# Attention rows of maxima sent per pair of heads, maxima of the first sixteen heads placed later

## The chip, the cores and the metric

The kernel runs on one core of a Trainium2 chip. The metric is the time of one execution on the device in microseconds (us); lower is better. Before the change three runs took 604.35, 604.46 and 606.38 us, so the median is 604.46 us.

## The reference

The input x has shape (4, 512, 128): 4 batches of 512 tokens of width 128. What is computed:

```
x  = x + attention(layernorm(x))         # its own two layer norms inside
x  = x + moe(layernorm(x))               # 8 experts, the best 2 of each token

attention(x):                            # 16 heads of 64, one shared key/value head
    xn = ln1(x);  q = xn @ Wq;  k, v = split(xn @ Wkv)
    sim  = q k^T * 64**-0.5              # per batch and head: 512 x 512
    attn = softmax(sim)                  # minus the row's maximum, exp, over the sum
    return ln2((attn v) @ Wo)
```

Only the attention's start is touched by the change: the row maxima of `sim` and how they reach the score matmul.

## The kernel before

All work of the attention is one list of steps, written by `attention_schedule`. Each step has a place (a slot number, then an order inside the slot), the list is sorted by it, and every engine walks the same list and issues only what is its own. So the list fixes the order of work inside each engine, and semaphores fix it between engines. The list counts 64 heads (4 batches of 16), 32 pairs of heads, and four tiles of 128 tokens to a head, so 256 slots. Slot n holds `EXP` n.

The steps around the change:

- `Q` p: TensorE makes the queries of pair p in one PSUM bank `q_ps` with three matmuls (high and low parts of a float32 split, L1205 to L1207). Batch steps `XT`, `K` and `V` use the same bank, and each of them waits until the one before has been read (`bank_read`).
- `QHI` p: ScalarE copies the rounded (high) part into `q_hl`, one instruction to each of the two heads (L1177). `QLO` p: VectorE writes the remainder (low part) into the other half of `q_hl`, two instructions (L1100). GpSimd copies the high parts once more, into `q_hm` (L1021).
- `MAX` k: TensorE multiplies one tile of 128 queries with all keys into one of two banks of `max_ps` (L1270) and VectorE takes the negated maximum over each row, a column of `less_max` (L1115). The matmul of `MAX` k waits until `MAX` k-2 has been reduced. There are four to a head; the first of a head waits for the head's `QLO`.
- `SHIFT` n: VectorE transposes a group's columns of `less_max` with four 32x32 transposes into `mrow` (L1126), and the DMA queue of SyncE writes them as row 64 of `q_hm` (L957), one DMA to a pair of heads. Behind each of the first nine `SHIFT` the same queue issues up to four large writes that blank `sorted_rows` in HBM (L963), which the experts' part needs later.
- `EXP` k: TensorE makes a 128x512 tile of scores with two matmuls, L1290 (from `q_hl`) and L1292 (from `q_hm`, which adds the row of maxima), and ScalarE takes the exponential (L1195). The first `EXP` of a group of heads waits for that group's row DMAs. The matmuls of `EXP` k wait until exponential k-2 is done (two banks of `s_ps`).
- `PV`: matmuls of `prob` with `v` (L1306, four records to a step). `V`, `VC`: values of a batch, made by TensorE and copied by ScalarE.
- `keep_busy`: matmuls on zeros into an unused bank (L1220) that feed nothing; one stands in front of each of `MAX` 2 to 11, five before `MAX` 0 and three before the first `V`.

`shifts` groups the heads: two groups of two heads, then groups of four. `less_max` has two buffers of 32 columns. In slot order the list of before around the start reads:

```
... Q0 QHI0 QLO0 MAX0-4 Q1 MAX5 QHI1 MAX6 MAX7 QLO1 SHIFT0 MAX8-11 Q2 QHI2 QLO2
EXP0 MAX12,13 EXP1 MAX14,15 EXP2 MAX16,17 SHIFT1 EXP3 MAX18,19 Q3 EXP4 MAX20,21 QHI3 QLO3
EXP5 MAX22,23 V VC EXP6 MAX24,25 PV EXP7 MAX26,27 Q4 EXP8 MAX28,29 PV QHI4 QLO4
EXP9 MAX30,31 PV EXP10 MAX32 EXP11 MAX33 PV SHIFT2 EXP12 ...
```

Of the kernel before, what the change touches and what calls it, by code (L numbers as in the profile page):

```python
# [5 lines left out]
F32 = mybir.dt.float32  # L6
# [6 lines left out]
P = 128  # L13
# [3 lines left out]
UH = 8  # L17
UP = UH // 2
JT = 4
# [8 lines left out]
def attention_schedule(units):  # L28

    slots, lead = UH * JT, MAX_LEAD
    placed = []

    def place(slot, order, kind, u, a):
        placed.append((slot, order, (kind, u, a)))

    for n, kind in enumerate(IN_STEPS):

        place(FIRST_V_AT if kind in ("V", "VC") else -1000 + n, 4, kind, 0, 0)
        for b in range(1, units // 2):

            place(2 * slots * (b - 1) + IN_AT[n] + (LATER if b == 1 else 0), 4, kind, b, 0)
    for b in range(units // 2 - 1):
        at, lag = (AFTER_AT, 2) if b < units // 2 - 2 else (LATE_AFTER_AT, 0.25)
        for n, kind in enumerate(AFTER_STEPS):
            place(2 * slots * (b + 1) + at[n], 4, kind, b, 0)  # L60
        for n in range(TOP_K * JT if b < units // 2 - 2 else EARLY_SENDS):
            place(2 * slots * (b + 1) + at[AFTER_STEPS.index("PLACE")] + lag * n, 4.5, "SEND", b, n)
    for pair in range(units * UP):
        u, p = divmod(pair, UP)

        at = (-30, -11, *FIRST_Q_AT)[pair] if pair < 4 else 8 * pair - 19 - lead
        place(at, 3, "Q", u, p)
        place(at + 1, 3, "QHI", u, p)

        place(-8 if pair == 1 else at + 1, 4, "QLO", u, p)  # L70
        for jt in range(JT):
            place(8 * pair + PV_AT[jt], 2, "PV", u, p * JT + jt)
        place(8 * pair + PV_AT[-1] + 1, 1, "RAW", u, p)
    for n in range(units * slots):
        u, a = divmod(n, slots)
        place(n, 0, "EXP", u, a)
        place(n - 15 if n < 12 else (n - 12) // 2 if n < 32 else n - 16 - lead, 1, "MAX", u, a)
    for n, (head, _) in enumerate(shifts(units)):
        place(FIRST_SHIFT_AT[n] if n < 2 else JT * head - lead + 1, 3, "SHIFT", n, 0)
    for u in range(units):  # L80
        after = slots * (u + 1)
        if u < units - 1:
            place(after + SUM_AT[0], 5, "SUM", u, 0)
            place(after + SUM_AT[1], 5, "SUM", u, 1)
            for n, kind in enumerate(RECIP_STEPS):
                place(after + RECIP_AT[n], 5, kind, u, 0)
            for c in range(UP):
                place(after + NORM_AT[c], 5, "NORM", u, c)
                place(after + NORM_AT[c] + OUT_LAG, 5, "OUT", u, c)
        else:  # L90

            for c, at in enumerate(LAST_SUM_AT):
                place(after + at, 6, "SUM", u, c)
            for n, (kind, a) in enumerate(LAST_STEPS):
                place(after + LAST_SUM_AT[1] + 1, 9 + n, kind, u, a)
    return [step for _, _, step in sorted(placed, key=lambda entry: entry[:2])]
# [27 lines left out]
LAST_STEPS = (("SUMS", 0), ("SPREAD", 0), ("RECIP", 0), ("GATHER", 0), ("NORM", 0), ("NORM", 1), ("OUT", 0),  # L124
              ("NORM", 2), ("OUT", 1), ("NORM", 3), ("OUT", 2), ("OUT", 3))

FIRST_Q_AT = (-3, 3)

FIRST_SHIFT_AT = (-7.5, 2)

FIRST_V_AT = 5

LATER = 8

VECTOR_HEADS = (7,)

# [5 lines left out]

def shifts(units):

    return [(0, 2), (2, 2)] + [(head, 4) for head in range(4, units * UH, 4)]


EXPERTS = 8  # L150
# [28 lines left out]
def bass_preln_mqa_moe_kernel(nc, x, ln1_g, ln1_b, wq, wkv, wo, ln2_g, ln2_b, gate_wT, gate_upT, downT,  # L179
# [32 lines left out]
    with ExitStack() as whole:  # L212
# [659 lines left out]
        with ExitStack() as att:  # L872
# [15 lines left out]
            wkl = sb(att, "wkl", [P, P], F32R)  # L888
            wvh = sb(att, "wvh", [P, DH], F32R)
            wvl = sb(att, "wvl", [P, DH], F32R)  # L890
            less_max = sb(att, "less_max", [P, 2, 32], F32R)
            mrow = sb(att, "mrow", [32, 2, P], F32R)
            prob = sb(att, "prob", [P, 4, JT, S])
            fold = sb(att, "fold", [P, 2, S])
# [28 lines left out]
            @block.sync  # L923
            def _(sp):
                sp.dma_start(x1[:, 0:TPB, :], x_t[0]).then_inc(x1_in[0], 16)
                for dst, src in ((ident[:, :], eye), (gcol[:, :], ln1_g.rearrange("(p o) -> p o", o=1)),
                                 (bcol[:, :], ln1_b.rearrange("(p o) -> p o", o=1)),
                                 (sumsel[:, :, :], sum_rows)):
                    sp.dma_start(dst, src).then_inc(consts_in, 16)
                sp.dma_start(wk_raw[:, 0:DH], wkv[:, 0:DH]).then_inc(wkv_in, 16)  # L930
                sp.dma_start(wk_raw[:, DH:P], wkv[:, 0:DH]).then_inc(wkv_in, 16)
                sp.dma_start(wv_raw, wkv[:, DH:2 * DH]).then_inc(wkv_in, 16)
                sp.dma_start(wq_raw, wq).then_inc(wq_in, 16)
                sp.dma_start(wof[:, :, :], wo.rearrange("(c p) n -> p c n", p=P)).then_inc(wo_in, 16)
                for half in range(2):
                    for part in range(2):
                        row = part * LOW_ROW + half * UH // 2
                        sp.dma_start(hs_raw[row:row + UH // 2, :, :],
                                     head_rows[half + 2 * part:P:32, :, :]).then_inc(hs_in, 16)
                for b in range(1, NB):  # L940
                    sp.dma_start(x1[:, b * TPB:(b + 1) * TPB, :], x_t[b]).then_inc(x1_in[b], 16)
                for dst, src in ((g2[:, :], ln2_g.partition_broadcast(P)), (b2[:, :], ln2_b.partition_broadcast(P)),
                                 (gw[:, :], gate_wT), (tri[:, :, :], lower)):
                    sp.dma_start(dst, src).then_inc(consts2_in, 16)
                for kind, u, a in steps:
                    tail_sync(sp, kind, u)
                    if kind == "SHIFT":
                        head, heads = shift_heads[u]

                        sp.wait_ge(mrow_ready, u + 1)  # L950
                        if head >= Q_SLOTS:

                            sp.wait_ge(score_mm, (head + heads - Q_SLOTS) * JT)
                        for h in range(0, heads, 2):
                            slot = (head + h) % Q_SLOTS
                            first = (head % 4 + h) * JT
                            sp.dma_start(q_hm[DH:DH + 1, slot:slot + 2, :].bitcast(F32),  # L957
                                         mrow[first:first + 2 * JT, u % 2, :].bitcast(F32)).then_inc(mrow_in[u % 2], 16)

                        if u == 0:  # L960
                            sp.wait_ge(blank_set, 1)
                        for n in range(4 * u, min(4 * u + 4, FILLS)):
                            sp.dma_start(sorted_rows[n * S:(n + 1) * S, :].rearrange("(p r) c -> p r c", r=TPB),  # L963
                                         blank[:, :, :]).then_inc(rows_filled, 16)
                    if kind == "V" and u == NB - 1:
                        sp.wait_ge(rows_filled, 16 * FILLS)
                        for e in range(E):
                            load_gate_up(sp, e)
                sp.wait_ge(tiles_ready, 1)
                sp.wait_ge(rows_sent, 16 * TOP_K * TPB * (LB - 1))  # L970
                for k in range(EARLY_ROWS):
                    load_rows(sp, k, xs_early[:, k, :])
# [88 lines left out]
            def _(dve):  # L1061
                nc.vector.memset(kly[DH:DH + 1, :, :].bitcast(F32), 1.0).then_inc(ones_set, 1)
                link(dve, nc.vector.memset(less_max[:, :, :].bitcast(F32), 0.0))
                for kind, u, a in steps:
# [38 lines left out]
                    if kind == "MAX":  # L1103
                        k = u * UH * JT + a
                        head, it = divmod(k, JT)
                        group, i = divmod(head, 4)
                        dve.wait_ge(max_mm, k + 1)
                        col = i * JT + it
                        if i == 0 and it == 0 and group >= 2:

                            dve.wait_ge(mrow_ready, group)
                        if head == 2 and it == 0:

                            dve.wait_ge(mrow_ready, 1)
                        nc.vector.tensor_reduce(less_max[:, group % 2, col:col + 1], max_ps[:, k % 2, :], AX_X,  # L1115
                                                ALU.max, negate=True).then_inc(max_done, 1)
                    if kind == "SHIFT":
                        head, heads = shift_heads[u]
                        group = head // 4
                        dve.wait_ge(max_done, (head + heads) * JT)  # L1120
                        if u >= 2:

# [1 line left out]
                        for n in range(P // 32):  # L1124
                            part = slice(32 * n, 32 * n + 32)
                            last = nc.vector.transpose(mrow[:, u % 2, part].bitcast(F32),  # L1126
                                                       less_max[part, group % 2, :].bitcast(F32))
                        last.then_inc(mrow_ready, 1)
                    if kind == "EXP" and a % JT >= 1 and vector_sums(u * UH + a // JT):

# [71 lines left out]
            def _(pe):  # L1202
# [23 lines left out]
                for kind, u, a in steps:  # L1226
# [33 lines left out]
                    if kind == "MAX":  # L1260
                        i, it = divmod(a, JT)
                        k = u * UH * JT + a
                        if it == 0:
                            pe.wait_ge(q_lo, u * UH + i + 1)
                        if 2 <= k < 12:
                            keep_busy(BUSY["rows"])
                        if k >= 2:

# [544 lines left out]
```

## Time and profile before

| | before |
|---|---|
| median of 3 runs | 604.46 us |
| profiled execution, its own time | 608.39 us |
| span of its trace | 606.6 us |
| mean granted TensorE clock | 0.984 of full speed |
| TensorE matmul busy | 571.6 us |
| VectorE busy | 398.2 us |
| ScalarE busy | 296.9 us |
| GpSimd busy | 395.7 us |

The profile's PE is TensorE's matmuls, PEld its weight loads, DVE is VectorE, ACT ScalarE, POOL GpSimd, and SPq the DMA queue of SyncE. PE's busy time is an outline of pipelined matmuls, so a busy PE may still lose time between them. PEclk 1.00 is the full clock of 2.4 GHz, 0.50 the half clock of 1.2 GHz.

### The profile page before, as it was taken

What the parts mean: (1) busy time and instruction counts of PE and PEld (TensorE: products, weight loads), DVE (VectorE), ACT (ScalarE), POOL (GpSimd) and SP (SyncE); (2) the same over time, 40 slices, a digit from 0 to 9 for tenths busy, and PEclk for the clock granted to TensorE, in tenths of its full rate; (3) what the DMA queues carried; (4) which work ended last, traced back from release to release, by engine and by line L of the source; (5) the groups of instructions that cost most, each with busy time, mean ns of one, the idle gap of its engine ahead of it and who ended that gap; (6) DMA issues with size and microseconds to landing.
All of it is one profiled execution on the core that took longest, in us unless ns stands there. A gap on an engine that the chain in (4) does not pass through costs nothing. (4 is left out here: it accounts for less than half of the span.)

```text
span 606.6 us, 8802 instructions
## 1 busy us (share of the span) xinstructions
PE 571.6 (94%) x2543; PEld 325.6 (54%) x2543; DVE 398.2 (66%) x873; ACT 296.9 (49%) x559; POOL 395.7 (65%) x329
## 2 busy tenths in 40 slices
PE   8799999999999999998999999899997878999992
PEld 6464455444545454444545445344433567788881
DVE  4878656657756869774676878875584468444453
ACT  3235655445636564553655455355536553444550
POOL 5438776667758866799696579849747934445333
PEclk9889999999999999999999999899999999999997
DMA  5111011010201200071000000000005300231033
GB/s 166 71 72 71 2 71 71 5 72 1 75 1 72 74 2 1 7 243 69 1 5 0 2 7 21 13 2 4 11 0 151 94 23 27 58 81 52 23 126 98
DMA packets 27518, 29.46 MB, mean 49 GB/s; under 512 B 7732, under 2 KB 18742, under 8 KB 27473
## 3 DMA queue, kind: packets, MB, share of 16 engines
q1 hardware_dynamic: 24912, 24.27, 12.6%
q0 software_dynamic: 2272, 4.24, 2.1%
q8 instruction: 23, 0.38, 0.3%
q10 hardware_dynamic: 288, 0.39, 0.2%
q14 instruction: 23, 0.18, 0.1%
HBM read 13.50 MB, written 15.32 MB: 48 GB/s over the span
## 5 line engine op out<-in xcount | busy, mean ns | idle before, releaser
L1195 ACT ACTIVATE prob<-s_ps 128x512 f32<-128x512 f32 x256 | 150.8, 599 | 183.3 <-PE s_ps L1292 180.7
L1115 DVE TENSOR_REDUCE less_max<-max_ps 128x1 fp32r<-128x512 f32 x256 | 174.0, 689 | 82.5 <-PE max_ps L1270 79.7
L1041 POOL TENSOR_TENSOR fold<-prob 128x1024 f32<-128x1024 f32 x63 | 149.9, 2380 | 88.3 <-ACT prob L1195 87.6
L1306 PE MATMUL pv_ps<-prob,v 128*64 128x512 f32 x512 | 138.5, 621 | 0.0
L1290 PE MATMUL s_ps<-q_hl,khh 128*128 128x512 f32 x256 | 117.9, 461 | 0.7 <-ACT prob L1195 0.7
L1270 PE MATMUL max_ps<-khh,q_hl 128*128 128x512 f32 x256 | 103.0, 408 | 5.3 <-DVE less_max L1115 4.7
L1292 PE MATMUL s_ps<-q_hm,kly 65*128 65x512 f32 x256 | 101.8, 398 | 0.0
L1290 PEld LDWEIGHTS s_ps<-q_hl,khh 128*128 128x128 f32 x256 | 48.6, 190 | 86.2 <-ACT prob L1195 67.0
L1047 POOL TENSOR_TENSOR psums<-fold 128x512 f32<-128x512 f32 x63 | 80.9, 1285 | 4.9
L1270 PEld LDWEIGHTS max_ps<-khh,q_hl 128*128 128x128 f32 x256 | 49.1, 192 | 23.4 <-DVE less_max L1115 11.0
L1292 PEld LDWEIGHTS s_ps<-q_hm,kly 65*128 65x128 f32 x256 | 48.8, 191 | 9.2 <-issue 3.4
L1306 PEld LDWEIGHTS pv_ps<-prob,v 128*64 128x64 f32 x512 | 25.6, 135 | 46.2 <-issue 34.5
L497 POOL DMA_INDIRECT sorted_rows<-xr,place_i x32 | 34.7, 1084 | 22.4 <-issue 12.7
L1100 DVE TENSOR_TENSOR q_hl<-q_ps,q_hl 64x512 fp32r<-64x512 f32 x64 | 44.1, 689 | 6.3 <-ACT q_hl L1177 4.9
L1514 DVE TENSOR_TENSOR ha<-up_ps,gl 128x512 f32<-128x512 f32 x39 | 26.9, 690 | 29.4 <-PE up_ps L1651 13.6
L1177 ACT ACTIVATE q_hl<-q_ps 64x512 fp32r<-64x512 f32 x64 | 37.6, 587 | 12.4 <-PE q_ps L1207 11.5
L1475 POOL DMA_INDIRECT parts<-raw,psums x22 | 22.2, 1011 | 29.1 <-DVE raw L1523 23.6
L787 DVE TENSOR_TENSOR ao<-sum_ps,raw 128x512 f32<-128x512 f32 x32 | 22.1, 690 | 27.2 <-PE sum_ps L853 27.1
L1021 POOL TENSOR_SCALAR q_hm<-q_hl 64x1024 fp32r<-64x1024 f32 x32 | 33.4, 1043 | 8.6 <-ACT q_hl L1177 8.6
L1588 ACT ACTIVATE ht<-q_ps 128x512 f32<-128x512 f32 x39 | 23.3, 597 | 27.2 <-PE q_ps L1660 24.5
L863 PE MATMUL y_ps<-ao,wof 128*128 128x512 f32 x64 | 35.9, 646 | 0.0
L1673 PE MATMUL sum_ps<-wd,ht 128*128 x216 | 29.2, 278 | 5.0 <-DVE raw L1523 2.7
(251 smaller groups left out, 769.8 us busy)
## 6 DMA issues: line engine op xcount, KB each, us to landing
sorted_rows<-raw_w SPq DMA_DIRECT2D x36, 260.0 KB, 2.6
raw_w<-in_gate_upT SPq DMA_DIRECT2D x8, 512.0 KB, 9.2
wd<-in_downT SPq DMA_DIRECT2D x8, 256.0 KB
raw_w<-parts SPq DMA_DIRECT2D x7, 256.0 KB, 3.2
psums<-sorted_rows SPq DMA_DIRECT2D x22, 65.0 KB, 1.7
x<-in_x SPq DMA_DIRECT2D x4, 256.0 KB, 4.4
xs_first<-sorted_rows SPq DMA_DIRECT2D x15, 65.0 KB, 1.8
out<-x SPq DMA_DIRECT2D x3, 256.0 KB, 2.3
```

The lines of the kernel that those rows point to most:

```text
L497: nc.gpsimd.indirect_dma_start(out=sorted_rows, out_offset=bass.IndirectOffsetOnAxis(ap=place_i[:, n, t:t + 1], axis=0), in_=xr[:, n, t, : ...
L863: nc.tensor.matmul(y_ps[:, :], wof[:, c, :], ao[:, k % 2, :], start=c == 0, stop=c == PAIRS - 1).then_inc(out_mm, 1)
L1041: nc.gpsimd.tensor_tensor(fold[:, :, :], prob[:, head % 4, 0:2, :], prob[:, head % 4, 2:4, :], ALU.add).then_inc(prob_folded, 1)
L1047: nc.gpsimd.tensor_tensor(psums[:, head % SUM_SLOTS, :], fold[:, 0, :], fold[:, 1, :], ALU.add).then_inc(head_sum, 1)
L1100: nc.vector.tensor_tensor(q_hl[DH:P, h % Q_SLOTS, :], q_ps[DH * hd:DH * hd + DH, :], q_hl[0:DH, h % Q_SLOTS, :].bitcast(F32), ALU.subtract ...
L1115: nc.vector.tensor_reduce(less_max[:, group % 2, col:col + 1], max_ps[:, k % 2, :], AX_X, ALU.max, negate=True).then_inc(max_done, 1)
L1177: nc.scalar.activation(q_hl[0:DH, (2 * k + hd) % Q_SLOTS, :], q_ps[DH * hd:DH * hd + DH, :], ACT.Copy).then_inc(q_hi, 1)
L1195: nc.scalar.activation(prob[:, head % 4, jt, :], s_ps[:, k % 2, :], ACT.Exp, scale=SCALE).then_inc(exp_done, 1)
L1270: nc.tensor.matmul(max_ps[:, k % 2, :], q_hl[:, k // JT % Q_SLOTS, it * P:(it + 1) * P], khh[:, b % 2, :], start=True, stop=True).then_inc ...
L1290: nc.tensor.matmul(s_ps[:, k % 2, :], khh[:, b % 2, keys], q_hl[:, slot, :], start=True, stop=False)
L1292: nc.tensor.matmul(s_ps[:, k % 2, :], kly[0:DH + 1, b % 2, keys], q_hm[0:DH + 1, slot, :], start=False, stop=True).then_inc(score_mm, 1)
L1306: last = nc.tensor.matmul(pv_ps[DH * hd:DH * hd + DH, :], v[:, b % 2, jt, :], prob[:, head % 4, jt, :], start=(jt == 0), stop=(jt == JT - 1))
```

## The change

- The first sixteen heads are shifted in eight groups of two (before: two, two, four, four, four). Later groups still hold four heads. `less_max` gets a third buffer, and each group takes the next one in turn.
- `MAX` 10 to 63 are placed at 0.78 of a slot each from slot 0 on. Before, `MAX` 12 to 31 stood two to a slot and one to a slot followed.
- `SHIFT` 0 now stands ahead of `QLO` 1 (the low parts of the second pair).
- `Q` 2 moves from before `EXP` 0 to behind it, `Q` 3 from slot 3 to 4, and `SHIFT` 1 from slot 2 to 4.5.
- The single `keep_busy` matmuls stand in front of `MAX` 2 to 9 only, two fewer.

```diff
-        place(-8 if pair == 1 else at + 1, 4, "QLO", u, p)
+        place(-7.4 if pair == 1 else at + 1, 4, "QLO", u, p)
...
-        place(n - 15 if n < 12 else (n - 12) // 2 if n < 32 else n - 16 - lead, 1, "MAX", u, a)
+        place(n - 15 if n < 10 else 0.78 * (n - 10) if n < 64 else n - 16 - lead, 1, "MAX", u, a)
...
-FIRST_Q_AT = (-3, 3)
+FIRST_Q_AT = (0, 4)
-FIRST_SHIFT_AT = (-7.5, 2)
+FIRST_SHIFT_AT = (-7.5, 4.5)
...
+MAX_SLOTS = 3
...
-    return [(0, 2), (2, 2)] + [(head, 4) for head in range(4, units * UH, 4)]
+    return [(head, 2) for head in range(0, 16, 2)] + [(head, 4) for head in range(16, units * UH, 4)]
...
-            less_max = sb(att, "less_max", [P, 2, 32], F32R)
+            less_max = sb(att, "less_max", [P, MAX_SLOTS, 32], F32R)
...
-                            first = (head % 4 + h) * JT
+                            first = h * JT
...
-                        group, i = divmod(head, 4)
+                        n = max(n for n, (first, _) in enumerate(shift_heads) if first <= head)
                         dve.wait_ge(max_mm, k + 1)
-                        col = i * JT + it
-                        if i == 0 and it == 0 and group >= 2:
-                            dve.wait_ge(mrow_ready, group)
-                        if head == 2 and it == 0:
-                            dve.wait_ge(mrow_ready, 1)
-                        nc.vector.tensor_reduce(less_max[:, group % 2, col:col + 1], max_ps[:, k % 2, :], AX_X,
+                        col = k - shift_heads[n][0] * JT
+                        if col == 0 and n >= MAX_SLOTS:
+                            dve.wait_ge(mrow_ready, n - MAX_SLOTS + 1)
+                        nc.vector.tensor_reduce(less_max[:, n % MAX_SLOTS, col:col + 1], max_ps[:, k % 2, :], AX_X,
...
-                                                       less_max[part, group % 2, :].bitcast(F32))
+                                                       less_max[part, u % MAX_SLOTS, :].bitcast(F32))
...
-                        if 2 <= k < 12:
+                        if 2 <= k < 10:
                             keep_busy(BUSY["rows"])
```

The list after the change reads:

```
... Q0 QHI0 QLO0 MAX0-4 Q1 MAX5 QHI1 MAX6 MAX7 SHIFT0 QLO1 MAX8,9
EXP0 MAX10 Q2 MAX11 EXP1 QHI2 QLO2 MAX12 EXP2 MAX13 EXP3 MAX14,15 EXP4 Q3 SHIFT1 MAX16
EXP5 QHI3 V VC QLO3 MAX17 EXP6 PV MAX18 EXP7 Q4 MAX19,20 EXP8 PV QHI4 QLO4 MAX21
EXP9 PV MAX22 EXP10 MAX23,24 EXP11 PV SHIFT2 MAX25 EXP12 ... SHIFT3 behind EXP19, SHIFT4
behind EXP27, SHIFT5 behind EXP35, SHIFT6 behind EXP43, SHIFT7 behind EXP51
```

From slot 42 on the two lists hold the same steps at the same places, but for the numbering of the shifts and one more shift of two heads in slot 51.

## Rows read from the trace of the kernel before

**Rows 1.** Busy time of each engine over the span.
```profile
PE 571.6 (94%) x2543; PEld 325.6 (54%) x2543; DVE 398.2 (66%) x873; ACT 296.9 (49%) x559; POOL 395.7 (65%) x329
```

**Rows 2.** By stretches: bounds, length, busy time (instructions) by engine, clock, DMA, GB/s.
```profile
20.00:30.00 10.00, 6.68 (x20) 4.30 (x18) 8.04 (x16) 2.61 (x5) 2.53 (x7) 0.83 0.28 107
30.00:40.00 10.00, 9.03 (x31) 5.88 (x31) 9.04 (x18) 3.51 (x7) 4.73 (x4) 0.83 0.24 91
...
160.00:200.00 40.00, 40.00 (x172) 20.92 (x168) 23.68 (x44) 20.27 (x39) 29.71 (x24) 1.00 0.08 28
```

**Rows 3.** Waits from 45 to 120 us: in total, times, longest.
```profile
PEld max_ps L1270 <- DVE less_max L1115: 0.2, 1, 0.2
```

**Rows 4.** Timeline of PE, 20 to 31 us: start, length, what [idle before].
```profile
20.37 0.49 PE L1270 MATMUL max_ps<-khh,q_hl 128*128 128x512 f32 x1
22.36 0.50 PE L1220 MATMUL y_ps<-q_hm 128*128 128x512 f32 x1 [1.50 <-DVE q_hl L1100]
...
24.75 0.80 PE L1270 MATMUL max_ps<-khh,q_hl 128*128 128x512 f32 x1 [0.96 <-DVE less_max L1115]
...
27.48 0.58 PE L1290 MATMUL s_ps<-q_hl,khh 128*128 128x512 f32 x1
...
28.59 0.39 PE L1290 MATMUL s_ps<-q_hl,khh 128*128 128x512 f32 x1
28.83 0.39 PE L1292 MATMUL s_ps<-q_hm,kly 65*128 65x512 f32 x1
30.53 1.28 PE L1270 MATMUL max_ps<-khh,q_hl 128*128 128x512 f32 x2 [1.32 <-DVE less_max L1115]
```

**Rows 5.** Timeline of DVE, 19 to 33 us.
```profile
19.63 1.97 DVE L1115 TENSOR_REDUCE less_max<-max_ps 128x1 fp32r<-128x512 f32 x3 [0.46 <-PE max_ps L1270]
21.63 1.41 DVE L1100 TENSOR_TENSOR q_hl<-q_ps,q_hl 64x512 fp32r<-64x512 f32 x2
23.07 0.84 DVE L1126 STREAM_TRANSPOSE mrow<-less_max 32x32 f32<-32x32 f32 x4
...
28.35 1.41 DVE L1100 TENSOR_TENSOR q_hl<-q_ps,q_hl 64x512 fp32r<-64x512 f32 x2 [1.21 <-ACT q_hl L1177]
29.79 2.75 DVE L1115 TENSOR_REDUCE less_max<-max_ps 128x1 fp32r<-128x512 f32 x4
```

**Rows 6.** Timeline of ACT, 27 to 31 us.
```profile
27.72 1.22 ACT L1177 ACTIVATE q_hl<-q_ps 64x512 fp32r<-64x512 f32 x2 [7.34 <-PE q_ps L1207]
28.96 1.08 ACT L1195 ACTIVATE prob<-s_ps 128x512 f32<-128x512 f32 x2
```

**Rows 7.** Row DMAs: issues on SPq, and the one score matmul released by them.
```profile
23.93 0.78 SPq L957 DMA_DIRECT2D q_hm<-mrow  x1
...
260.43 1.38 SPq L957 DMA_DIRECT2D q_hm<-mrow  x2
...
264.19 0.19 PEld L1290 LDWEIGHTS s_ps<-q_hl,khh 128*128 128x128 f32 x1 [0.19 <-DMA q_hm<-mrow]
```

**Rows 8.** Stretches of 1 us, the clock's column third from the end.
```profile
24.00:25.00 1.00, 0.25 (x1) 0.25 (x2) 0.99 (x2) 0.00 (x0) 0.00 (x0) 0.73 0.00 0
...
27.00:28.00 1.00, 1.00 (x4) 0.77 (x3) 0.13 (x1) 0.28 (x1) 0.00 (x0) 0.57 0.99 383
...
31.00:32.00 1.00, 0.91 (x3) 0.72 (x3) 0.92 (x3) 0.00 (x0) 0.00 (x0) 0.64 0.00 0
...
34.00:35.00 1.00, 1.00 (x4) 0.65 (x4) 0.96 (x5) 0.59 (x1) 0.00 (x0) 0.65 0.03 8
```

**Rows 9.** Timeline of PE, 39 to 40 us, the first V.
```profile
39.27 0.30 PE L1205 MATMUL q_ps<-wvh,xh 128*128 128x64 f32 x1 [0.24 <-DVE q_hl L1100]
```

**Rows 10.** Timeline of PE, 379 to 392 us: an idle time and the same PV behind it.
```profile
379.33 1.08 PE L1306 MATMUL pv_ps<-prob,v 128*64 128x512 f32 x4
...
388.13 0.50 PE L1270 MATMUL max_ps<-khh,q_hl 128*128 128x512 f32 x1 [1.55 <-DVE less_max L1115]
...
390.12 1.97 PE L1306 MATMUL pv_ps<-prob,v 128*64 128x512 f32 x4
```

More of the change, by code:

```diff
@@ L1118, in _ @@
                         head, heads = shift_heads[u]
-                        group = head // 4
                         dve.wait_ge(max_done, (head + heads) * JT)
```

## The prediction

> **What bounds the kernel now.** I read the busy shares first, then the stretches, then the waits of the start, and then the timeline of each engine there. PE is busy 94% of the span and no other engine over 66% [rows 1]. From 40 us on the stretches are full, as in 160 to 200 us, where PE shows 40.00 of 40.00 while DVE has 23.68 [rows 2], and between 45 and 120 us PE waits for a maximum only once, for 0.2 us [rows 3]. There the attention's length is the sum of PE's instructions, and moving maxima about inside it changes nothing. The start is different. From 20 to 30 us PE has 6.68 us of work in 10, and the granted clock is 0.83 in both stretches from 20 to 40 us [rows 2]. So the change can win or lose only what PE idles or runs at half clock in the start, and whatever it shifts there moves all that follows.
>
> The idle times are three. PE stops at 20.86 us and waits 1.50 us for QLO 1, then 0.96 us for a reduction, then 1.32 us for the reduction of MAX 12, which stands behind QLO 2 [rows 4, 5]. A short one of 0.24 us precedes the first V, which waits for QLO 3 to free the bank [rows 9]. Behind the first two the clock falls: 0.73 in the microsecond from 24 and 0.57 in that from 27 make a stretch of half clock (1.2 GHz) from about 24.5 to 27.9 us. Behind the third comes one from about 31.3 to 34.7 us (0.64 and 0.65 at its ends) [rows 8]. A third case late in the trace says the same: 1.55 us of idle time, and the PV behind it takes 1.97 us in place of 1.08 [rows 10].
>
> **Prices.** A 512-column matmul takes PE 0.24 us from start to start at full clock (28.59 to 28.83) [rows 4], and by the ratio of the two PVs, 1.97 / 1.08, some 0.43 us at half clock [rows 10]. From an EXP's first matmul to its exponential is 0.24 + 0.39 (the length of the second one) + 0.04 = 0.67 us. A reduction costs DVE 0.66 us (1.97 / 3), a QLO 1.41 us, a SHIFT 0.84 us [rows 5], a QHI 1.22 us of which the first half lets QLO start after 0.63 (27.72 to 28.35), an exponential 0.6 us [rows 6]. After a wait PE starts some 0.05 us behind the releaser.
>
> **The change, part by part.** Up to MAX 7, reduced at 21.60 (19.63 + 1.97), both lists are alike. All times below are on the trace's clock.
>
> *SHIFT 0 ahead of QLO 1.* DVE transposes from 21.63 to 22.47, so the row DMA is issued at about 22.49 in place of 23.93: 1.44 us earlier. QLO 1 follows from 22.50 and its first half ends at 23.20 in place of 22.33. PE waits for just that, so the idle time from 20.86 grows from 1.50 to 2.37 us. Then come two maxima with their keep-busy matmuls until 24.26.
>
> *EXP 0 early.* It needs the DMA's landing, which the trace of before hides: EXP 0 was not held up there, its weight load coming at most 3.1 us after the issue. The one release by such a DMA came at 264.18, and of the two issued from 260.43 the second began about 0.69 us in, so 3.06 us later [rows 7]. Bounds are therefore 0 and 3.1 us, and I take 3.06, the only one seen: EXP 0 at 25.55, in place of 27.48. PE idles 1.3 us more.
>
> The Trainium skill's page "DMA: Bandwidth & Descriptors", section "Anatomy of one DMA", gives about 2.0 us of fixed cost to a DMA, mostly completion. By an estimate from that page EXP 0 would start at 24.5; the row above (3.06 us) disagrees, and I go by the row.
>
> *Q2 behind EXP 0, QHI 2 behind exponential 1.* Here ACT's order matters: it takes EXP 0, EXP 1 and only then QHI 2, where before QHI 2 came first. With the half clock lying where it lay in the trace, PE issues EXP 0, MAX 10, Q2, MAX 11 until 28.3 and EXP 1 at 28.3. Exponential 1 ends at 28.3 + 0.67 + 0.6 = 29.55, QLO 2 starts 0.63 later at 30.2 and ends at 31.6, and the reduction of MAX 12 ends at 32.3. MAX 14 waits for that one. PE has MAX 12, EXP 2, MAX 13 and EXP 3 between (six matmuls), is done at 30.15 and idles 2.2 us, in place of 1.32.
>
> *Q3 later, V at its old place.* Between Q3 and V now stand only MAX 16, EXP 5 and the three keep-busy matmuls; before, it was EXP 4, EXP 5, four maxima and the three. QHI 3 stands behind exponential 5. From EXP 5's first matmul, e, QLO 3 ends at e + 0.67 + 0.6 + 0.63 + 1.41 = e + 3.3; PE has 0.47 of EXP 5 and 0.7 of keep-busy, so it idles 2.15 us where before it idled 0.24. From 32.35 PE does MAX 14, MAX 15 (after one more reduction, 0.65), EXP 4, Q3, MAX 16: eight matmuls, so e = 34.7 at full clock and V at 38.05. A half clock of 3.4 us over this, as before had one, costs 0.2 us on each of five to eight matmuls and puts V at 39.1.
>
> *What is still owed at V.* Before, 24 maxima were done when V started at 39.27, now 17. Seven matmuls of 0.235, or 1.65 us, are still to come in a stretch where PE is the bound. So V breaks even at 39.27 - 1.65 = 37.6. The result is +0.45 us with one fall of the clock, +1.5 with two. A third fall behind the gap before V would slow V (12 matmuls of 64 columns) and the next few, by 1.0 at most, so +2.5.
>
> *Maxima at 0.78 of a slot, slots 10 to 42.* DVE gets 10.25 maxima in 8 slots (6.8 us), a QLO and a SHIFT, 9.1 us. PE has 8 EXPs of 0.47, 10.25 maxima of 0.24, four PVs of 1.08 and a Q of 0.7, 11.3 us. That is covered by PE on average. Where a SHIFT, the statistics of batch 1 and no PV fall together, PE may wait a few tenths: 0 to 1 us in sum, taken as 0.
>
> *Three more shifts.* 3 x 0.84 = 2.5 us of DVE, beside a PE-bound stretch, where DVE has 16 us idle in 40 [rows 2]. Nothing; without cover the whole 2.5. *Row DMAs* are as many as before, and the blanking writes come with earlier shifts, behind the row DMA of their own group and 8 slots (over 10 us) ahead of the next. *Two keep-busy matmuls fewer* are in the sums above: 0.47 us off PE, all of it in idle time. *The third buffer* and its waits are for DVE's own earlier transposes: nothing.
>
> **Sum.** I take the case of two falls, less the little that a shorter DMA gives back: +1.3 us. For the profiled execution, 608.39 us, that makes 609.7. Its median stands 3.93 us lower, and the same shift gives 604.46 + 1.3 = 605.8 us.
>
> **The rivals.**
>
> *The clock holds (faster).* EXP matmuls now come sooner behind MAX 9, and the clock may not fall. Then nothing is run at half clock: with Q2 and EXP 1 at 0.24 a matmul EXP 1 starts at 27.0 instead of 28.3, V at 36.7, so -0.9; with the rows landing 1 us sooner -1.6, and 0.25 more where before still waited for DVE at slots 6 to 10. It decides from the point where PE's idle time before 24.3 us is not followed by a clock under 1. For it: 9 reductions fewer (5.9 us of DVE) before EXP 10, where DVE had 9.04 of 10 us [rows 2]. Against it: each idle time of 1.3 us or more of PE was followed by a fall [rows 4, 8, 10], and the new ones are longer. That is about -1.5, so 603.0 us. At the far end the seven maxima still owed (1.65 us) go into gaps between PE's steps and cost nothing: 601.3.
>
> The Trainium skill's page "TensorE: Matmul & The Clock Gate", section "Terms", prices half clock as half of its duration. By that page two stretches of 3.4 us would be an estimated 3.4 us lost, where I count the matmuls that run in them (before: 7 or 8 times 0.2 us each). The rows agree only where PE is full.
>
> *DVE becomes the bound in slots 10 to 42, with three falls (slower).* VectorE at 9.1 us in 8 slots bunches behind SHIFT and QLO, costing 1 to 2 us on top of +2.5. For it: PE waits for the second last reduction, so any 2.25 us of QLO plus SHIFT is felt. Against: PV steps of 1 us stand between. It gives 608.0.
>
> *The change does nothing measurable.* The losses and gains cancel to within 0.3 us: 604.5.
>
> **How the numbers follow.** Forecast (one or two falls) 0.42, clock holds 0.26, DVE bound or third fall 0.20, nothing 0.12. A difference counts from 0.5%, 3.0 us. Forecast and cancellation lie wholly inside. Of the faster rival 0.10 lies beyond, of the slower one 0.14. The range of 601.9 to 608.1 leaves out the far ends of both rivals; the likeliest case alone spans 604.9 to 607.0.
>
> **What the profile after would show.** A SHIFT at 21.6 and its DMA at 22.5 us; a keep-busy matmul behind 2.4 us of idle time; EXP 0 near 25.5, released by the DMA; QHI 2 behind two exponentials; idle times of about 2 us on PE before MAX 14 and before V; clock under 1 behind each. V starting before 37.6 us at full clock would prove me wrong, as would waits of PE for maxima over 1 us in sum between 45 and 75 us, or a gain over 3 us from anywhere behind slot 42.

## The result: 0.9% slower

The changed kernel takes 610.45 us (median of 5 runs, 609.25 to 613.08) against 604.46 us before (5 runs, 603.58 to 606.38). The ratio is 1.0093, with a 95% interval of 1.0069 to 1.0116 (it is estimated over all executions; the plain quotient of the medians is 1.0099): 6 us slower. The direction was forecast, the size was not (+1.3 us), and the time lies above the range's end of 608.1.

The profiled execution of the changed kernel took 612.22 us, its trace spans 610.4 us, the mean granted clock is 0.979 in place of 0.984. It is the execution with the lowest clock of the five: the others have 0.982 to 0.985, by which (twice the difference times the span) they ran some 4 to 7 us less at half clock. Line numbers moved by one or two: L1268 is now the matmul of a maximum, L1288 and L1290 those of a score, L1218 the keep-busy one, L1102 `QLO` and L1114 the reduction. In the experiments' kernels they move again.

Busy times hardly moved, which answers [rows 1]: the same work was done, later.

```profile
PE 572.8 (94%) x2541; PEld 326.8 (54%) x2541; DVE 401.3 (66%) x885; ACT 298.1 (49%) x559; POOL 396.8 (65%) x329
```

The stretches show where, against [rows 2] (bounds, length, busy time by engine, clock, DMA, GB/s). The clock is 0.66 and 0.75 where it was 0.83 and 0.83, PE has 6.82 us of work from 30 to 40 us in place of 9.03, and half clock reaches past 40 us.

```profile
20.00:30.00 10.00, 7.50 (x19) 5.58 (x19) 6.21 (x13) 2.65 (x5) 0.56 (x2) 0.66 0.28 107
30.00:40.00 10.00, 6.82 (x23) 5.26 (x23) 5.96 (x12) 2.96 (x6) 5.41 (x4) 0.75 0.28 109
40.00:50.00 10.00, 10.00 (x32) 4.79 (x32) 4.31 (x7) 3.84 (x7) 3.67 (x3) 0.74 0.00 0
```

PE's timeline answers [rows 4] and [rows 9]. The three idle times are there: 2.38 us before MAX 8, 1.74 us before MAX 14, 1.91 us before V. (This execution reached MAX 7 1.30 us earlier, so 21.95 here is 23.25 on the clock of before.)

```profile
21.95 0.80 PE L1218 MATMUL y_ps<-q_hm 128*128 128x512 f32 x1 [2.38 <-DVE q_hl L1102]
...
23.82 0.63 PE L1288 MATMUL s_ps<-q_hl,khh 128*128 128x512 f32 x1
...
31.19 1.39 PE L1268 MATMUL max_ps<-khh,q_hl 128*128 128x512 f32 x2 [1.74 <-DVE less_max L1114]
...
38.18 0.30 PE L1203 MATMUL q_ps<-wvh,xh 128*128 128x64 f32 x1 [1.91 <-DVE q_hl L1102]
...
42.18 1.98 PE L1304 MATMUL pv_ps<-prob,v 128*64 128x512 f32 x4
...
46.53 0.39 PE L1288 MATMUL s_ps<-q_hl,khh 128*128 128x512 f32 x1
```

The three stretches at half clock reach from 21.3 to 28.1, from 31.5 to 34.9 and from 38.4 to 45.2 us, 17 us in all, where [rows 8] had 6.8 us in two. Their borders are read from stretches of 1 us (the clock is third from the end; a mean of 0.65 is 0.7 us at half clock):

```profile
21.00:22.00 1.00, 0.05 (x1) 0.05 (x1) 0.94 (x3) 0.00 (x0) 0.00 (x0) 0.65 0.00 0
...
28.00:29.00 1.00, 1.00 (x5) 0.77 (x4) 0.00 (x0) 0.98 (x3) 0.00 (x0) 0.94 0.00 0
...
31.00:32.00 1.00, 0.73 (x2) 0.40 (x3) 0.98 (x3) 0.00 (x0) 1.00 (x1) 0.77 0.00 0
...
34.00:35.00 1.00, 1.00 (x4) 0.71 (x3) 0.19 (x1) 0.07 (x1) 0.52 (x1) 0.53 0.00 0
...
38.00:39.00 1.00, 0.82 (x5) 0.82 (x5) 0.12 (x1) 0.00 (x0) 0.42 (x1) 0.68 0.64 252
...
45.00:46.00 1.00, 1.00 (x5) 0.77 (x5) 0.61 (x1) 0.43 (x1) 0.00 (x0) 0.91 0.00 0
```

### The profile page after: what moved, and what is told of

Same layout as the page of the kernel before. It is cut to its first block and busy times, and to the rows that moved or that the text cites. A ratio compares the mean times of both kernels' runs of the same rounds, so it can differ in the third digit from the quotient of the medians.

```text
span 610.4 us, 8817 instructions
## 1 busy us (share of the span) xinstructions
PE 572.8 (94%) x2541; PEld 326.8 (54%) x2541; DVE 401.3 (66%) x885; ACT 298.1 (49%) x559; POOL 396.8 (65%) x329
## 3 DMA queue, kind: packets, MB, share of 16 engines
HBM read 13.50 MB, written 15.32 MB: 47 GB/s over the span
## 5 line engine op out<-in xcount | busy, mean ns | idle before, releaser
L1114 DVE TENSOR_REDUCE less_max<-max_ps 128x1 fp32r<-128x512 f32 x256 | 174.1, 689 | 83.5 <-PE max_ps L1268 81.1
L1288 PE MATMUL s_ps<-q_hl,khh 128*128 128x512 f32 x256 | 116.3, 454 | 0.7 <-ACT prob L1193 0.7
L1268 PE MATMUL max_ps<-khh,q_hl 128*128 128x512 f32 x256 | 106.7, 420 | 5.5 <-DVE less_max L1114 4.7
L1290 PE MATMUL s_ps<-q_hm,kly 65*128 65x512 f32 x256 | 102.4, 400 | 0.0
L1288 PEld LDWEIGHTS s_ps<-q_hl,khh 128*128 128x128 f32 x256 | 49.2, 192 | 70.3 <-ACT prob L1193 52.2
L1049 POOL TENSOR_TENSOR psums<-fold 128x512 f32<-128x512 f32 x63 | 82.3, 1307 | 4.9
L1268 PEld LDWEIGHTS max_ps<-khh,q_hl 128*128 128x128 f32 x256 | 49.4, 194 | 39.5 <-DVE less_max L1114 21.8
L1290 PEld LDWEIGHTS s_ps<-q_hm,kly 65*128 65x128 f32 x256 | 49.1, 192 | 10.4 <-issue 3.3
L1102 DVE TENSOR_TENSOR q_hl<-q_ps,q_hl 64x512 fp32r<-64x512 f32 x64 | 44.1, 690 | 10.1 <-ACT q_hl L1175 8.8
```

The costliest lines, as they stand in the source:

```text
L1049: nc.gpsimd.tensor_tensor(psums[:, head % SUM_SLOTS, :], fold[:, 0, :], fold[:, 1, :], ALU.add).then_inc(head_sum, 1)
L1102: nc.vector.tensor_tensor(q_hl[DH:P, h % Q_SLOTS, :], q_ps[DH * hd:DH * hd + DH, :], q_hl[0:DH, h % Q_SLOTS, :].bitcast(F32), ALU.subtract ...
L1114: nc.vector.tensor_reduce(less_max[:, n % MAX_SLOTS, col:col + 1], max_ps[:, k % 2, :], AX_X, ALU.max, negate=True).then_inc(max_done, 1)
L1268: nc.tensor.matmul(max_ps[:, k % 2, :], q_hl[:, k // JT % Q_SLOTS, it * P:(it + 1) * P], khh[:, b % 2, :], start=True, stop=True).then_inc ...
L1288: nc.tensor.matmul(s_ps[:, k % 2, :], khh[:, b % 2, keys], q_hl[:, slot, :], start=True, stop=False)
L1290: nc.tensor.matmul(s_ps[:, k % 2, :], kly[0:DH + 1, b % 2, keys], q_hm[0:DH + 1, slot, :], start=False, stop=True).then_inc(score_mm, 1)
```

## A ledger that all runs can be laid on

Executions reach the start at slightly different times, so each trace is read from one event: the end of MAX 7's reduction, up to which the lists are alike. From there, the start of the n-th exponential in ACT's timeline (us). The first four columns come from one profiled execution to each kernel, the medians from 5 executions of the changed kernel and 6 to 12 of each experiment:

| | EXP 6 | EXP 12 | EXP 48 | EXP 64 | median us | ratio to before, interval |
|---|---|---|---|---|---|---|
| before | 19.78 | 30.44 | 84.72 | 112.13 | 604.46 | 1 |
| changed | 21.99 | 33.97 | 92.39 | 119.79 | 610.45 | 1.0093 (1.0069 to 1.0116) |
| changed, idle times filled (e1) | 16.61 | 27.23 | 85.67 | 113.08 | 606.82 | 1.0032 (1.0016 to 1.0049) |
| changed, fill before V only (g2) | 17.82 | 28.43 | 86.86 | 114.26 | 608.02 | 1.0055 (1.0033 to 1.0076) |
| changed, Q back (e3) | 15.32 | 25.94 | 84.35 | 111.76 | 606.46 | 1.0030 (1.0016 to 1.0044) |
| e3, filled (h1) | 14.72 | 25.35 | 83.78 | 111.18 | 606.03 | 1.0014 (0.9992 to 1.0037) |
| changed, maxima back (e4) | 21.22 | 33.14 | 87.43 | 114.84 | 608.30 | 1.0067 (1.0043 to 1.0091) |
| e4, filled (g1) | 19.81 | 30.49 | 84.79 | 112.18 | 607.07 | 1.0035 (1.0015 to 1.0055) |
| e1, maxima apart (h3) | 15.91 | 26.45 | 83.67 | 111.07 | 606.34 | 1.0019 (0.9996 to 1.0042) |
| pairwise shifts only (e2) | 19.75 | 30.46 | 84.74 | 112.14 | 605.73 | 1.0009 (0.9991 to 1.0028) |
| before, shift first (f2) | 18.92 | 29.63 | 83.91 | 111.33 | 605.21 | 0.9999 (0.9982 to 1.0016) |
| before, filled (f3) | 17.84 | 28.52 | 82.83 | 110.22 | 604.29 | 0.9988 (0.9965 to 1.0010) |
| f2, filled (h2) | 17.84 | 28.52 | 82.83 | 110.24 | 604.03 | 0.9991 (0.9968 to 1.0015) |
| f3, Q 3 a slot later (h4) | 19.75 | 31.96 | 86.26 | 113.65 | 607.75 | 1.0054 (1.0029 to 1.0078) |

In the experiments the kernel before had medians of 605.25 to 605.51 us, and each ratio is against these, not against 604.46. "Filled" means keep-busy matmuls, which feed nothing, put into the idle times. The difference is made by EXP 48: 92.39 - 84.72 = 7.67 us, of which 3.53 by EXP 12. (The spans differ by 3.8 us. The changed kernel's execution was 1.30 us ahead at MAX 7, and that of before lost 1.5 us between EXP 152 and the last exponential, where its clock fell at 390 us, [rows 10]. The last 1.1 us lie behind the attention and are not explained.)

## The experiments

The theories: *the clock* (matmuls run at half clock behind the idle times), *the late maxima* (a bill that is paid in slots 12 to 48), *the pairwise shifts*.

**e1: the changed kernel, idle times filled.** One line ahead of the waits of MAX 8 and MAX 14, and ten keep-busy matmuls in place of three before V.

```diff
-BUSY = {"start": 20, "K": 8, "MAX": 5, "V": 3, "rows": 1}
+BUSY = {"start": 20, "K": 8, "MAX": 5, "V": 10, "rows": 1}
+FILL = {8: 9, 14: 7}
...
+                        keep_busy(FILL.get(k, 0))
                         if it == 0:
                             pe.wait_ge(q_lo, u * UH + i + 1)
```

> The changed kernel with its three new idle times of TensorE filled by keep-busy matmuls: nine ahead of MAX 8, seven ahead of MAX 14, ten in place of three ahead of the first V; no order is changed. Clock theory (the 6 us are matmuls run at half clock behind those idle times, 17 us of half clock in the changed kernel's trace before 46 us against 6.8 us before the change): the clock stays at 1.00 or nearly, and 3.5 to 5 us come back, 605.5 to 607.0 us. Theory of the late maxima or of the pairwise shifts: nothing comes back, 610 us or a little more, since PE has the same waits and more to do.

606.82 us, within the clock theory's bounds. The trace of e1 in stretches shows the clock held:

```profile
20.00:30.00 10.00, 9.13 (x37) 6.22 (x36) 8.28 (x16) 3.35 (x6) 2.70 (x3) 1.00 0.28 109
30.00:40.00 10.00, 9.73 (x46) 6.98 (x47) 5.21 (x11) 3.85 (x7) 3.81 (x4) 1.00 0.28 107
```

Matmuls that compute nothing gave back 6.74 us at EXP 12 (33.97 to 27.23), and 3.6 us of the whole time (610.45 to 606.82; the two intervals don't overlap). They add work and change no order, so what they gave back is the clock. How the two numbers differ is told in the part on the prediction. EXP 12 now comes 3.2 us sooner than before the change, and still the kernel is slower: from EXP 12 to EXP 48 it takes 58.4 us in place of 54.3. That is the second part of the bill.

**e2: only the pairwise shifts are left of the change.** The order, the keep-busy matmuls and the first two shifts are those of before.

```diff
-        place(-7.4 if pair == 1 else at + 1, 4, "QLO", u, p)
+        place(-8 if pair == 1 else at + 1, 4, "QLO", u, p)
...
-        place(n - 15 if n < 10 else 0.78 * (n - 10) if n < 64 else n - 16 - lead, 1, "MAX", u, a)
+        place(n - 15 if n < 12 else (n - 12) // 2 if n < 32 else n - 16 - lead, 1, "MAX", u, a)
...
-FIRST_Q_AT = (0, 4)
-FIRST_SHIFT_AT = (-7.5, 4.5)
+FIRST_Q_AT = (-3, 3)
+FIRST_SHIFT_AT = (-7.5, 2)
...
-                        if 2 <= k < 10:
+                        if 2 <= k < 12:
```

> The changed kernel with the whole order of before (maxima, Q, low parts, first two shifts, keep-busy) and only the eight shifts of two heads and the third buffer left of the change. Clock theory: 604.5 us, within 1 us of before. Theory of the pairwise shifts (three more transposes on VectorE, blanking writes earlier): 606 us or more.

605.73 us against 605.25, and the ledger of before to 0.03 us up to EXP 64: up to there the pairwise shifts and their earlier blanking writes are free, as predicted. In the whole time the interval (0.9991 to 1.0028) leaves room for up to 1.7 us; see the last section.

**e3: the changed kernel with Q 2 and Q 3 where they were.**

```diff
-FIRST_Q_AT = (0, 4)
+FIRST_Q_AT = (-3, 3)
```

> The changed kernel with Q 2 and Q 3 back at their slots of before (-3 and 3). QHI 2 then stands ahead of exponential 0, and EXP 4 again between Q 3 and V. Clock theory with its two gaps (before MAX 14 and before V) made by the place of Q: both gaps shrink under 1.3 us, the third stretch of half clock goes, and 3 to 5 us come back, 605.5 to 607.5 us. Late maxima or pairwise shifts as the cause: 610 us.

606.46 us: two numbers in one line return 4 us. In e3's timeline of PE the idle times for a reduction (0.59 us where it was 1.74) and before V (0.81 where it was 1.91) have shrunk, and in the start of e3's trace the clock falls once only, behind the first one, for 3.4 us. Up to EXP 64 this execution is even 0.4 us ahead of before, while the median is 1.2 us above; the trace has a fall at 276.9 us that the one of before has not.

```profile
23.27 0.50 PE L1218 MATMUL y_ps<-q_hm 128*128 128x512 f32 x1 [2.38 <-DVE q_hl L1102]
...
28.70 0.47 PE L1268 MATMUL max_ps<-khh,q_hl 128*128 128x512 f32 x1 [0.59 <-DVE less_max L1114]
...
34.60 0.30 PE L1203 MATMUL q_ps<-wvh,xh 128*128 128x64 f32 x1 [0.81 <-DVE q_hl L1102]
```

**e4: the changed kernel with the maxima of before.**

```diff
-        place(n - 15 if n < 10 else 0.78 * (n - 10) if n < 64 else n - 16 - lead, 1, "MAX", u, a)
+        place(n - 15 if n < 12 else (n - 12) // 2 if n < 32 else n - 16 - lead, 1, "MAX", u, a)
...
-FIRST_SHIFT_AT = (-7.5, 4.5)
+FIRST_SHIFT_AT = (-7.5, 2)
...
-                        if 2 <= k < 10:
+                        if 2 <= k < 12:
```

> The changed kernel with the maxima placed as before (two to a slot up to slot 9) together with their keep-busy matmuls and SHIFT 1 in slot 2; Q, the low parts and the pairwise shifts stay as changed. Theory of the late maxima: this returns most of the 6 us, 605 to 606 us. Clock theory: the gaps made by Q and by the low parts stay, but more maxima stand in them, so part of it comes back, 607 to 609 us.

608.30 us, as the clock theory expected. The idle time ahead of MAX 16 is 1.39 us and no fall follows; the one before V is followed by 3.4 us of half clock. EXP 12 comes almost as late as in the changed kernel (33.14), since the idle time before V stays (1.88 us), but slots 12 to 48 take 54.3 us again.

**f2: the kernel before with SHIFT 0 ahead of QLO 1.**

```diff
-        place(-8 if pair == 1 else at + 1, 4, "QLO", u, p)
+        place(-7.4 if pair == 1 else at + 1, 4, "QLO", u, p)
```

> The kernel before with one edit: SHIFT 0 ahead of QLO 1. Clock theory: the idle time before MAX 8 grows from 1.5 to 2.4 us and the rows leave 1.4 us sooner, but EXP 0 still stands behind Q 2; some 0.5 to 1 us slower than before at most, 605.3 to 606.3 us, with two stretches of half clock as before. If the swap is what costs the 6 us: 608 us or more.

605.21 us, no difference; my lower bound was a little too high. PE waits 2.37 us in place of 1.50 and 0.96, but no longer stops again before MAX 10. The two stretches of half clock that I expected did not both come: the clock falls behind the 2.37 us for 3.4 us, and stays at 1.00 behind the 1.45 us before MAX 14.

**f3: the kernel before, filled** (`FILL = {8: 6, 10: 3, 14: 5}`, `"V": 3`).

> The kernel before with its three idle times filled by keep-busy matmuls: six ahead of MAX 8, three ahead of MAX 10, five ahead of MAX 14. Clock theory: no half clock in the start (6.8 us in the trace of before), matmuls that ran at 0.43 us run at 0.24 us, 2 to 3 us faster than before, 602.3 to 603.3 us. If half clock is only a companion of waits for VectorE: 605 us, no change.

604.29 us against 605.51: 1.2 us, and the interval (0.9965 to 1.0010) includes 1. A miss in the whole time; in the ledger it is 1.9 us at each mark from EXP 6 on, and in its trace the clock stays at 1.00 through the start.

**g1: e4, filled** (`FILL = {8: 9, 16: 6}`, `"V": 10`).

> The changed kernel with the maxima placed as before (and their keep-busy matmuls, SHIFT 1 in slot 2) and with its idle times filled: nine ahead of MAX 8, six ahead of MAX 16, ten ahead of the first V. Against the run with the late maxima and filled idle times (606.8 us) it shows what the late maxima cost at full clock. Theory that they cost 3.6 us in slots 12 to 48 and give 2.7 us before: 604 to 605 us. If they cost nothing at full clock: 606.5 to 607.5 us.

607.07 us, in the bounds of "they cost nothing". In the ledger, EXP 48 is at 84.79 against 85.67 in e1: at full clock the late maxima cost 0.9 us net, which the whole time does not show.

**g2: the changed kernel with `"V": 10` alone.**

> The changed kernel with seven more keep-busy matmuls ahead of the first V alone; the idle times before MAX 8 and MAX 14 stay. Clock theory, with the stretch of half clock behind the idle time before V (about 7 us long, over V, EXP 6, a PV and EXP 7) as the costliest: 2.5 to 3.5 us come back, 607 to 608 us. My prediction's price of at most 1.0 us for it: 609.5 us.

608.02 us: at the clock theory's end and not at mine. In the ledger EXP 12 comes 5.5 us sooner, more than the one filled idle time can give. Of that, 2.4 us are there at EXP 5, up to which the two kernels run the same steps: in g2's profiled execution the first fall lasted 3.4 us in place of 6.8, and the idle time before MAX 14 (1.92 us) was followed by none. The other 3.1 us come between V and EXP 8, where g2 has no half clock. So g2 shows 3.1 us for the filled wait, and 2.4 that are the difference of two executions.

```profile
22.43 0.50 PE L1220 MATMUL y_ps<-q_hm 128*128 128x512 f32 x1 [2.38 <-DVE q_hl L1104]
...
30.70 1.09 PE L1271 MATMUL max_ps<-khh,q_hl 128*128 128x512 f32 x2 [1.92 <-DVE less_max L1116]
```

In stretches:

```profile
20.00:30.00 10.00, 6.41 (x20) 4.33 (x19) 7.15 (x15) 3.14 (x6) 1.51 (x2) 0.83 0.28 107
30.00:40.00 10.00, 8.93 (x41) 6.17 (x42) 5.97 (x12) 3.46 (x7) 4.94 (x4) 1.00 0.28 109
```

**h1: e3, filled** (`FILL = {8: 9, 12: 2}`, `"V": 5`).

> The changed kernel with Q 2 and Q 3 back at slots -3 and 3 and its idle times filled: nine keep-busy matmuls ahead of MAX 8, two ahead of MAX 12, five ahead of the first V. Clock theory: no half clock; against the same order without filling (606.5 us, one stretch of 3.4 us) 1 to 1.5 us less, 605.0 to 605.5 us, EXP 64 at 110.5 us behind the reduction of MAX 7. If the late maxima's waits decide: 606.5 us.

606.03 us, between the two; EXP 64 at 111.18, 0.6 us before e3. Inconclusive in the whole time.

**h2: f2, filled** (`FILL = {8: 9, 14: 5}`).

> The kernel before with SHIFT 0 ahead of QLO 1 and its idle times filled: nine keep-busy matmuls ahead of MAX 8, five ahead of MAX 14. The candidate for a version faster than both. Clock theory: as the kernel before with filled idle times, 604.3 us, or up to 0.5 us less; 603.8 to 604.5 us. If the swap costs by its longer wait even at full clock: 605 us.

604.03 us against 605.37, 0.9991 (0.9968 to 1.0015). Its ledger is that of f3. It is the lowest median of all, and no measurement here tells it from the kernel before.

**h3: e1 with two maxima of one slot put apart,** one ahead of the slot's PV and one behind it. A maximum that has its slot to itself moves ahead of the PV too.

```diff
+def late_max(n):
+    at = 0.78 * (n - 10)
+    return int(at) if n == 10 or int(at) != int(at - 0.78) else int(at) + 0.5
...
-        place(n - 15 if n < 10 else 0.78 * (n - 10) if n < 64 else n - 16 - lead, 1, "MAX", u, a)
+        place(n - 15 if n < 10 else late_max(n) if n < 64 else n - 16 - lead, 1, "MAX", u, a)
```

> The changed kernel with filled idle times (nine, seven, ten), and where two maxima fall in one slot, the first is put ahead of the slot's PV and the second behind it, so that they are not back to back. Theory that PE's extra 1.7 us between EXP 12 and EXP 48 are waits of the second maximum of a pair for VectorE: EXP 12 to EXP 48 takes 57.2 us or less in place of 58.4, and the whole 1 us less than 606.8, 605.8 us. If they are the price of any maximum in that place: no difference, 58.4 and 606.8 us.

EXP 12 to EXP 48 takes 57.2 us in place of 58.4, as the theory of the pairs' waits asked. The whole is 606.34 us in place of the 605.8 expected; a possible reason is in the last section. Two of the seven pairs stay back to back, in slots without a PV. The waits from 45 to 120 us, of which [rows 3] had 0.2, show the same: they are waits of the weight loads, which overlap PE, so their sum is more than PE loses. First the changed kernel, then h3:

```profile
PEld max_ps L1268 <- DVE less_max L1114: 13.8, 20, 0.8
```

```profile
PEld max_ps L1276 <- DVE less_max L1121: 2.5, 5, 0.8
```

The two timelines of PE show the pair: in the changed kernel, from the first of two maxima to the next score 0.89 us (56.59 to 57.48),

```profile
55.58 1.08 PE L1304 MATMUL pv_ps<-prob,v 128*64 128x512 f32 x4
56.59 1.05 PE L1268 MATMUL max_ps<-khh,q_hl 128*128 128x512 f32 x2
57.48 0.39 PE L1288 MATMUL s_ps<-q_hl,khh 128*128 128x512 f32 x1
```

and in h3 a maximum alone takes 0.23 us, and 0.32 to 0.34 us right ahead of a PV or behind it.

```profile
55.90 0.50 PE L1276 MATMUL max_ps<-khh,q_hl 128*128 128x512 f32 x1
56.24 0.39 PE L1296 MATMUL s_ps<-q_hl,khh 128*128 128x512 f32 x1
...
56.70 0.39 PE L1276 MATMUL max_ps<-khh,q_hl 128*128 128x512 f32 x1
56.94 0.39 PE L1296 MATMUL s_ps<-q_hl,khh 128*128 128x512 f32 x1
```

**h4: f3 with Q 3 one slot later.**

```diff
-FIRST_Q_AT = (-3, 3)
+FIRST_Q_AT = (-3, 4)
```

> The kernel before with its idle times filled (six, three, five) and Q 3 one slot later, at slot 4, as in the change: QLO 3 then ends later and the first V waits for it. Theory that this wait and its half clock are the costliest part: an idle time of 1 to 2 us before V, a stretch of half clock behind it, and 2 to 4 us over the same kernel with Q 3 in slot 3 (604.3 us), 606.3 to 608.3 us. If more maxima in between cover it or the clock holds: 604.5 to 605.5 us.

607.75 us, 3.5 us over f3's 604.29: one step moved by one slot. EXP 12 is 3.44 us later. h4's timeline has the 1.88 us of idle time before V and, at half clock from 40.5 to 43.9 us, a PV of 1.98 us:

```profile
38.43 0.30 PE L1207 MATMUL q_ps<-wvh,xh 128*128 128x64 f32 x1 [1.88 <-DVE q_hl L1102]
...
41.17 1.98 PE L1309 MATMUL pv_ps<-prob,v 128*64 128x512 f32 x4
...
46.22 1.08 PE L1309 MATMUL pv_ps<-prob,v 128*64 128x512 f32 x4
```

## Why the prediction was wrong

**Right: where the idle times come.** Predicted 2.37, 2.2 and 2.15 us; measured 2.38, 1.74 and 1.91. The chains behind them (QLO 1 behind SHIFT 0, QHI 2 behind two exponentials, QHI 3 behind EXP 5 so that V waits for QLO 3) are those the trace shows, and h4 shows the last one by itself.

**Wrong: the price of the half clock, and the third fall left out.** This is the step that failed. The sum took two falls, the second at 1.05 us (V from 38.05 to 39.1), and left out a third behind the idle time before V, which the slower rival priced at 1.0 at most. Up to V the sum held: V came at 38.18, or 39.48 on the clock of before, where my forecast was 39.1. Behind V it broke: from V to EXP 8 the changed kernel takes 46.53 - 38.18 = 8.35 us, the kernel before 44.48 - 39.27 = 5.21, with the same four maxima in between. So the third fall cost 3.14 us where the sum had nothing. The runs price it: the same steps take 5.20 to 5.24 us in the ten traces at full clock there, 6.79 in e4 and 6.75 in h4, which have 3.4 us of half clock in them, and 8.35 with 6.8 us. So 3.4 us at half clock cost 1.55 us where PE is full, and h4 shows that a `Q` 3 one slot later is enough for it.

*How much of the 6 us it is.* At EXP 12 the changed kernel loses 6.74 us against e1, which has its order at full clock; the kernel before loses 1.92 against f3. The difference, 4.8 us, is the half clock's share of the 7.67 in these traces. It is too high for the changed kernel as a rule. Its first stretch lasted 6.8 us, where g2, e3, e4 and f2 have 3.4 us behind the same idle time of 2.37 or 2.38, and its clock is the lowest of its five executions. In the whole times, each against its own before, the changed kernel is at +6.0 us, e1 at +1.6 and f3 at -1.2, which leaves the clock some 3 us, with 1 to 5 allowed by the intervals.

**Wrong: "maxima at 0.78 of a slot, 0 to 1 us, taken as 0".** Between EXP 12 and EXP 48 the changed kernel takes 4.14 us more. All eight traces with the maxima where they were take 54.3 us there, and all five with them at 0.78 take 58.4. Eight maxima are owed at EXP 12 (1.9 us; at V it was seven, as counted). The rest, 2.2 us, I had averaged away: DVE has time enough in 8 slots, but 0.78 puts two maxima into about every fourth slot. Seven such pairs stand back to back, four of them behind a PV, and with two banks the second of a pair waits for a reduction. These seven took 0.71 us on average up to the next score (0.47 to 0.89) in place of 0.47, so 1.65 us. h3, with five of the seven apart, gets 1.2 us back. Some 0.6 us stay unexplained. The sign that I had named, waits of PE for maxima over 1 us between 45 and 75 us, came in the view of [rows 3] (6.3 us in 10 waits of PEld) and not in PE's own waits (0.2 us), where the second maximum's wait hides in busy time.

**The rest of the bill, at full clock.** At full clock the changed order reaches EXP 12 1.29 us before that of before (27.23 against 28.52, e1 and f3), and takes 4.13 us more than f3 after it, the owed maxima among them: net +2.84 us at EXP 48. With the clock's 4.83 us this makes the 7.67 of these traces. Of the 2.84, the maxima's places are 0.9 (e1 against g1) and the places of Q 2 and Q 3 with what is left of the change 1.96 (g1 against h2).

**The row DMA** was bounded by 0 and 3.1 us and put at 3.06. In the changed kernel it held nothing up: issued at 21.20, EXP 0 came at 23.82 right behind MAX 9, at most 2.6 us later. Where EXP 0 was released by it, in e1, it was issued at 21.45 and the matmul came at 23.59: 2.1 us.

```profile
21.45 0.78 SPq L961 DMA_DIRECT2D q_hm<-mrow  x1
```

That is e1's issue, and this its release, on PE:

```profile
23.59 0.47 PE L1291 MATMUL s_ps<-q_hl,khh 128*128 128x512 f32 x1 [0.19 <-DMA q_hm<-mrow]
```

So the one row of before misled; that other issues close to it made it longer is a guess. The Trainium skill's page "DMA: Bandwidth & Descriptors", section "Anatomy of one DMA", has about 2.0 us fixed, fitted for DMAs that GpSimd issues. This one is SyncE's, and the 2.1 us of this trace agree.

**The rivals.** "The clock holds" did not come; e1 shows what it would have been: not faster, 606.8. It was argued down with "each idle time of 1.3 us or more of PE was followed by a fall", and that is not so even in the trace of before: PE idles 1.64 us up to 275.64, and the clock stays at 1.00. "DVE becomes the bound with three falls" was nearest, with the right place and two of the right causes, at 608.0 still too low. My forecast took the mild case of each; here all three falls came, two of them twice as long as those of before, and the pairs' waits with them. The length was this execution's bad luck; that a third could come behind an idle time of 2.15 us was foreseen and left out.

## What to carry to other kernels

Where PE waits in a start, price the wait as the idle time plus the work behind it at half clock, here 1.55 us for each 3.4 us of it, and count each such wait as one that may bring a fall. One trace doesn't tell how long the stretch is: behind the same idle time of 2.38 us it was 3.4 us in g2 and 6.8 us in the changed kernel. Compare the mean clock of all executions with that of the profiled one before a trace is used for the size. Filling idle times with matmuls that feed nothing is a cheap test that separates the wait from the clock: here it gave back 6.7 us by EXP 12, and 3.6 us of the whole, without changing the order. When work is spread "at a rate", look at the pattern that rounding makes of it, since two buffers forgive one step and not two in a row.

## What the runs showed of the hardware

The same idle time does not always cost the clock. In the start, 1.32 us (before) and 1.42 us (e2) ahead of MAX 14 were followed by a fall, and 1.45 us (f2) and 1.92 us (g2) were not. Later, before the key matmuls of the fourth batch PE waits for GpSimd, 1.65 us in f2 (until 273.69) and 1.67 us in h3 (until 274.17). In f2 the clock stays at 1.00:

```profile
276.00:277.00 1.00, 1.00 (x5) 0.49 (x3) 0.64 (x2) 0.00 (x0) 1.00 (x1) 1.00 0.00 0
277.00:278.00 1.00, 1.00 (x5) 0.64 (x4) 0.34 (x1) 0.00 (x0) 0.92 (x2) 1.00 0.00 0
```

In h3, behind the same idle time, it falls:

```profile
276.00:277.00 1.00, 1.00 (x4) 0.00 (x0) 1.00 (x2) 0.23 (x1) 1.00 (x1) 0.50 0.03 4
277.00:278.00 1.00, 1.00 (x3) 0.50 (x2) 0.12 (x1) 0.00 (x0) 0.92 (x2) 0.50 0.00 0
```

From EXP 144 to EXP 152 f2 takes 16.5 us and h3 18.2 us, so the fall costs 1.7 us. EXP 144 to 152 takes the longer time in the profiled executions of e2, e3, g1, h1 and h3 (all with pairwise shifts), the shorter in those of the changed kernel, e1, e4 and g2 (with them too), and of before, f2, f3, h2 and h4. So five of nine kernels with pairwise shifts have it and none of five without them, too few executions to tell whether the shifts make it more frequent; that is a rival for the 0.5 us of e2 and for e3's 1.2 us, and was not tried.

Such falls fit the spread of 3 to 7 us between executions of one kernel, and that differences of 1 to 2 us in the ledger (f3, h1, h3) did not come out in the medians. In each of the twelve experiments the executions with a lower mean clock are the longer ones, with correlations of time and clock from -0.84 to -0.95 (f3 without one execution at 0.942). In h1 the five executions at 0.992 or more take 604.15 to 605.42 us, and the three at 0.987 take 608.65 to 609.31. What decides whether the clock falls was not shown.
